# A third up bank for a transformer layer with 64 experts, its opening in another order, and four norms moved to VectorE

## What is computed

```
e    = [fine[id], softmax(cluster logits[id] + b) @ coarse]        # 64 + 64 features
x1   = layernorm(e);  xn = rmsnorm(x1)
x2   = x1 + s1 * (decayed causal q k' v over the 512 tokens) o     # linear attention
h2   = e + x2 + s2 * gelu(rmsnorm(x2) read mix + bias) write       # two residuals
x3   = layernorm(h2)
gate = top 6 of softmax(x3 router), normalised; an expert takes at most 768 tokens in all
y    = h2 + mean of 2 shared experts(x3) + sum over 64 experts of gate * expert(x3)
expert(x) = (silu(x gate_w) * (x up_w)) down_w                     # 128 -> 64 -> 128
```

## Time and profile before

| | |
|---|---|
| median of three runs | 720.69 us |
| profiled execution, its own time | 720.98 us |
| its span in the trace | 719.1 us |
| TensorE products busy | 686.6 us, 95% |
| VectorE busy | 538.4 us, 75% |
| ScalarE busy | 450.4 us, 63% |
| GpSimd busy | 414.8 us, 58% |

### The profile page before, as it was taken

The page is one execution under the profiler, slowest core; times in us unless marked ns, Lnnn a source line. Parts: engine busy times, 40 slices in busy tenths (PEclk is TensorE's granted clock), DMA queues, the critical chain, the costliest instruction groups (busy, mean ns, idle before and its releaser), DMA issues.

```text
span 719.1 us, 10657 instructions
## 1 busy us (share of the span) xinstructions
PE 686.6 (95%) x3264; PEld 549.3 (76%) x3264; DVE 538.4 (75%) x1191; ACT 450.4 (63%) x790; POOL 414.8 (58%) x344
## 2 busy tenths in 40 slices
PE   8877998999999999999999999999999999999998
PEld 7766776788777877778777887778777788778885
DVE  5767689878778787887778787787878776786665
ACT  3345575576675676666765766766766747745554
POOL 5035567565655766565665656557575446556563
PEclk9989999999999999999999999999999999999999
DMA  5402543243223433333332533334332333344441
GB/s 199 167 1 94 159 126 106 93 141 111 103 90 114 127 112 99 113 111 103 114 108 80 147 111 97 111 113 120 112 97 101 114 112 115 94 116 132 140 125 51
DMA packets 49018, 80.54 MB, mean 112 GB/s; under 512 B 9537, under 2 KB 13761, under 8 KB 48961
## 3 DMA queue, kind: packets, MB, share of 16 engines
q1 hardware_dynamic: 47936, 77.76, 34.3%
q0 software_dynamic: 1024, 2.10, 1.6%
HBM read 76.68 MB, written 3.15 MB: 111 GB/s over the span
## 4 chain that ended last, share of the span: by engine, by line
PE 53%; DVE 15%; issue 14%; POOL 13%; ACT 2%; DMA 1%; POOLq 0%; DVEq 0%
POOL hid L1119 11%; PE bank_u L497 5%; PE bank_u L499 5%; PE bank_u L498 5%; PE bank_y L490 5%; PE bank_y L488 5%; PE bank_y L487 5%; PE bank_g L498 5%; PE bank_g L499 5%; PE bank_g L497 5%; DVE bank_u L965 3%; DVE hid_lo L971 3%; DVE taken L905 1%; POOL inv L1096 1%; PE bank_f L425 1%
## 5 line engine op out<-in xcount | busy, mean ns | idle before, releaser
L1119 POOL TENSOR_TENSOR hid<-hid,gate_rows 128x512 f32<-128x512 f32 x256 | 335.3, 1312 | 250.0 <-ACT hid L680 240.1
L688 ACT ACTIVATE hid_hi<-bank_u 128x512 fp32r<-128x512 f32 x259 | 154.6, 597 | 209.0 <-DVE bank_u L965 204.2
L971 DVE TENSOR_TENSOR hid_lo<-bank_u,hid_hi 128x512 fp32r<-128x512 f32 x259 | 178.0, 687 | 96.7 <-ACT hid_hi L688 93.6
L965 DVE TENSOR_TENSOR bank_u<-hid,bank_u 128x512 f32<-128x512 f32 x259 | 178.7, 690 | 47.7 <-PE bank_u L499 39.6
L680 ACT ACTIVATE hid<-bank_g 128x512 f32<-128x512 f32 x264 | 157.3, 596 | 4.3 <-PE bank_g L499 4.0
L497 PE MATMUL bank_u<-x_hi,up_hi 128*128 128x512 f32 x264 | 116.8, 442 | 13.2 <-DVE hid_lo L971 13.1
L497 PE MATMUL bank_g<-x_hi,gate_hi 128*128 128x512 f32 x264 | 106.6, 404 | 0.2 <-issue 0.2
L498 PE MATMUL bank_g<-x_hi,gate_lo 128*128 128x512 f32 x264 | 104.8, 397 | 0.0
L499 PE MATMUL bank_u<-x_lo,up_hi 128*128 128x512 f32 x264 | 104.8, 397 | 0.0
L498 PE MATMUL bank_u<-x_hi,up_lo 128*128 128x512 f32 x264 | 104.5, 396 | 0.0
L499 PE MATMUL bank_g<-x_lo,gate_hi 128*128 128x512 f32 x264 | 104.2, 395 | 0.0
(11 more groups left out here) (223 smaller groups left out, 820.9 us busy)
## 6 DMA issues: line engine op xcount, KB each, us to landing
gate_rows<-gates_dram SPq DMA_DIRECT2D x512, 128.0 KB, 2.9
out_dram<-later SPq DMA_DIRECT2D x7, 256.0 KB, 3.1
hid<-gate_t_dram SPq DMA_DIRECT2D x2, 704.0 KB, 5.8
gates_dram<-gates_t SPq DMA_DIRECT2D x8, 128.0 KB, 2.2
gate_rows<-up_t_dram SPq DMA_DIRECT2D x1, 704.0 KB, 5.6
later<-up_t_dram SPq DMA_DIRECT2D x1, 704.0 KB, 8.6
...
```

The source lines that it names most:

```text
L688: act.activation(hid_hi[:, split_slot(b, p), :], bank_u[(PAIRS * b + p) % 2][:, :], ACT.Copy)\
L965: dve.tensor_tensor(u, h, u, ALU.mult).then_inc(sem("product"), 1)
L971: dve.tensor_tensor(hid_lo[:, k, :], bank_u[(PAIRS * b + p) % 2][:, :], hid_hi[:, k, :].bitcast(F32), ALU.subtract).then_inc(sem("hid_lo"), 1)
L1119: pool.tensor_tensor(hid[:, s, :], hid[:, s, :], gate_rows[:, row, :], ALU.mult).then_inc(sem("gated"), 1)
```

## The change

- Banks: three `bank_u`, one `bank_y`. `up` of pair p waits for `hid_lo` of pair p - 3. The first down product of a batch waits until ScalarE has copied out the sum of the batch before; that copy stands at the start of ScalarE's pair 3 (it stood at pair 5), and at pair 3 TensorE's gate product stands ahead of its down product.
- Norms: `xn`, `x1`, `xn2` and `x3` of every batch are made by VectorE, four tensor_scalar instructions each, as batch 0's were; `scaled` is gone. GpSimd's offsets are still made.
- Opening: the down chunk 0 gets a buffer of its own, is loaded with the first, and is split at pairs 3 and 5 of batch 0; the last up chunk is loaded in its place later. Pair 0 is taken unsplit too (`LATE` = 6). GpSimd halves the shared experts' part behind `inv3`. TensorE does gates 0 to 3 and ups 0 to 2 before the gate transposes, and the transposes of `xn` of batch 1 ahead of them; VectorE does the products of pairs 0 and 1 and `xn` of batch 1 ahead of the token scan. In batch 0 the front-end stages 0 to 7 are done in pairs 0 to 3 (`DENSE`), and gates up to pair 7 and ups up to pair 5 are issued there.
- `hx` on GpSimd is two instructions of half the size, at pairs 12 and 13; `x1` shares memory with weights no longer needed.

```diff
--- before.py
+++ after.py
@@ -45,7 +45,7 @@
 SPLIT_RING = 3
-LATE = 5
+LATE = 6
@@ -57,9 +57,9 @@
              exp_t=9, coarse=10)
-ACT_AT = dict(xn=(-2, -1), xn_hi=0, x1=(1, 3), y_hi=2, z=4, ffn_t=5, xn2=(11, 12), xn2_t=13, vals=14, x3=(19, 20),
-              x3_hi=21, router_exp=23, cluster_exp=8, exp_t=10)
-POOL_AT = dict(inv2=10, hx=12, inv3=18, inv1=17)
+ACT_AT = dict(xn_hi=0, y_hi=2, z=4, ffn_t=3, xn2_t=13, vals=14, x3_hi=21,
+              router_exp=23, cluster_exp=8, exp_t=10)
+POOL_AT = dict(inv2=10, hx=(12, 13), inv3=18, inv1=17)
@@ -74,22 +74,24 @@
           ("up", 0, "rows", -20, 7),
-          ("gate", CHUNK, "hid1", 1, 10),
-          ("up", CHUNK, "later", 3, PAIRS + 3),
+          ("gate", CHUNK, "hid1", 1, 11),
+          ("up", CHUNK, "later", 3, PAIRS + 4),
           ("gate", 2 * CHUNK, "own0", 3, PAIRS + 14),
-          ("up", 2 * CHUNK, "own1", 5, PAIRS + 18),
-          ("down", 0, "rows", 10, 12),
+          ("down", 0, "own1", PAIRS + 3, PAIRS + 5),
+          ("up", 2 * CHUNK, "own1", PAIRS + 16, PAIRS + 18),
...
 FIRST_LOADS = 6
-RELOADS = {6: (1, None), 7: (3, 6), 8: (4, 17)}
+RELOADS = {6: (5, 7), 7: (3, 6), 8: (4, 17)}
...
 SHIFT = 7
-AHEAD = 3
-
-
-WARM = {-1: 8, 1: 12, 3: 9, 5: 7, 7: 36, 12: 3, 13: 4, 17: 24, PE_AT["gates_t"]: 6}
-WARM_START, WARM_PREP, WARM_EXP, WARM_COARSE, WARM_GATES = 20, (2, 9), 4, 26, 20
+AHEAD = 4
+GATES_BEFORE = 8
+DENSE = {0: (0, 1), 1: (2, 3), 2: (4, 5), 3: (6, 7), 4: (), 5: (), 6: (), 7: ()}
+
+
+WARM = {-1: 8, 1: 12, 3: 9, 5: 7, 7: 36, 12: 3, 13: 4, 17: 24}
+WARM_START, WARM_PREP, WARM_EXP, WARM_COARSE, WARM_GATES = 20, (2, 9), 4, 26, 8
@@ -225,9 +226,10 @@
         bank_g = [bank(f"bank_g{i}") for i in range(2)]
-        bank_u = [bank(f"bank_u{i}") for i in range(2)]
-        bank_y = [bank(f"bank_y{i}") for i in range(2)]
+        bank_u = [bank(f"bank_u{i}") for i in range(3)]
+        bank_y = bank("bank_y")
         bank_f = [bank(f"bank_f{i}") for i in range(2)]
+        bank_s = [bank_y, bank_u[2]]
@@ -242,11 +244,15 @@
-            return b == 0 and 1 <= p <= LATE
+            return b == 0 and p < LATE
...
-            return PAIRS * b + p + 1 - (LATE if b or p else 0)
+            return PAIRS * b + p + 1 - LATE
+
+        def stages(b, p):
+
+            return DENSE.get(p, (p,)) if b == 0 else (p,)
@@ -470,16 +475,20 @@
+            if b and p == 0:
+                pe.wait_ge(sem("ffn_t"), b)
...
                 pe.wait_ge(sem("h"), 2)
-            if b == 0 and p % CHUNK == 0:
-                pe.wait_ge(sem(f"split_lo{CHUNK_OF['down', p]}"), 1)
-            y = bank_y[b % 2][:, :]
+            if b == 0 and p in (LATE, CHUNK, 2 * CHUNK):
+                pe.wait_ge(sem(f"split_lo{CHUNK_OF['down', p // CHUNK * CHUNK]}"), 1)
+            y = bank_y[:, :]
             if is_late(b, p):
-                if p == 1:
-                    pe.wait_ge(sem("late_down"), 16)
-                pe.wait_ge(sem("gated"), gated_count(b, p))
-                pe.matmul(y, late_down[:, p - 1, :], hid[:, slot(b, p), :], start=False, stop=False)\
+                if p == 0:
+                    pe.wait_ge(sem("shared_down"), 2)
+                    pe.wait_ge(sem("late_up"), 1)
+                else:
+                    pe.wait_ge(sem("gated"), gated_count(b, p))
+                pe.matmul(y, late_down[:, p, :], hid[:, slot(b, p), :], start=(p == 0), stop=False)\
@@ -506,12 +515,12 @@
-            q, old = PAIRS * b + p, before(b, p, 2)
+            q, old = PAIRS * b + p, before(b, p, 3)
             if old and is_late(*old):
-                pe.wait_ge(sem("late_up"), old[1])
+                pe.wait_ge(sem("late_up"), old[1] + 1)
...
                 pe.wait_ge(sem("hid_lo"), split_count(*old))
-            expert_in(pe, "up", bank_u[q % 2][:, :], b, p)
+            expert_in(pe, "up", bank_u[q % 3][:, :], b, p)
@@ -523,23 +532,38 @@
             for p in range(PAIRS):
-                if p >= AHEAD or not first:
+                if p >= LATE or not first:
                     up(pe, b, p)
+                g = p + GATE_AHEAD
+                if p == LAG and not first:
+                    gate(pe, b, g)
                 if p >= LAG:
-                    down(pe, b, p - LAG)
+                    if not (first and p == LAG):
+                        down(pe, b, p - LAG)
...
                     down(pe, b - 1, p - LAG + PAIRS)
-                g = p + GATE_AHEAD
-                if AHEAD <= g < PAIRS or (g < AHEAD and not first):
+                if GATES_BEFORE <= g < PAIRS or (g < GATES_BEFORE and p != LAG and not first):
...
                     pe_out(pe, b - 1)
-                if late:
-                    pe_late(pe, b + 1, 1 - par, p, early)
+                if first and p == 0:
+                    gate(pe, 0, 4)
+                    up(pe, 0, 4)
+                    gate(pe, 0, 5)
+                elif first and p == 1:
+                    up(pe, 0, 5)
+                    gate(pe, 0, 6)
+                    down(pe, 0, 0)
+                elif first and p == 2:
+                    gate(pe, 0, 7)
+                for q in stages(b, p):
+                    if late:
+                        pe_late(pe, b + 1, 1 - par, q, early)
+                    if early:
+                        pe_early(pe, b + 2, q)
                 if early:
-                    pe_early(pe, b + 2, p)
@@ -593,14 +617,16 @@
                         up(pe, 0, k)
-                    warm(pe, bank_y[1], WARM_GATES)
+                    gate(pe, 0, AHEAD - 1)
+                    pe.wait_ge(sem("h"), 2)
+                    warm(pe, bank_y, WARM_GATES)
+                    pe.wait_ge(sem("router_logits"), 1)
+                    pe_late(pe, 1, 1, PE_AT["xn_t"], False)
...
                 if p == PE_AT["gates_t"]:
-                    gate(pe, 0, AHEAD - 1)
                     up(pe, 0, AHEAD - 1)
-                pe_early(pe, 1, p - SHIFT, bank_y)
-                warm(pe, bank_y[1] if p >= PE_AT["gates_t"] else bank_u[1], WARM.get(p, 0))
-            pe_late(pe, 1, 1, PE_AT["xn_t"], False)
+                pe_early(pe, 1, p - SHIFT, bank_s)
+                warm(pe, bank_u[1], WARM.get(p, 0))
@@ -612,30 +638,8 @@
-        def scaled(act, dst, src, scale, offset, half):
-
-            for t in (2 * half, 2 * half + 1):
-                if offset is None:
-                    last = act.activation(dst[:, t, :], src[:, t, :], ACT.Copy, scale=scale[:, t:t + 1])
-                else:
-                    last = act.activation(dst[:, t, :], src[:, t, :], ACT.Identity, bias=offset[:, t:t + 1],
-                                          scale=scale[:, t:t + 1])
-            return last
-
...
             f0, f1 = bank_f
-            if b and p in ACT_AT["xn"]:
-
-                act.wait_ge(sem("inv1"), b + 1)
-                scaled(act, xn, emb[par], inv1[:, 1, :], off1[:, 1, :], ACT_AT["xn"].index(p)).then_inc(sem("xn"), 1)
-            if b and p in ACT_AT["x1"]:
-                scaled(act, x1, emb[par], inv1[:, 0, :], off1[:, 0, :], ACT_AT["x1"].index(p)).then_inc(sem("x1"), 1)
-            if b and p in ACT_AT["xn2"]:
-                act.wait_ge(sem("inv2"), b + 1)
-                scaled(act, xn2, x2, inv2[:, :], None, ACT_AT["xn2"].index(p)).then_inc(sem("xn2"), 1)
-            if b and p in ACT_AT["x3"]:
-                act.wait_ge(sem("inv3"), b + 1)
-                scaled(act, x3, h2[par], inv3[:, :], off3[:, :], ACT_AT["x3"].index(p)).then_inc(sem("x3"), 1)
@@ -684,32 +688,34 @@
             if old >= 0:
-                act.wait_ge(sem("down_done"), old + (LATE if old else 0) + 1)
-            act.activation(hid_hi[:, split_slot(b, p), :], bank_u[(PAIRS * b + p) % 2][:, :], ACT.Copy)\
+                act.wait_ge(sem("down_done"), old + LATE + 1)
+            act.activation(hid_hi[:, split_slot(b, p), :], bank_u[(PAIRS * b + p) % 3][:, :], ACT.Copy)\
...
-        def act_copy_out(act, b, par):
+        def act_copy_out(act, b):
             act.wait_ge(sem("down_done"), PAIRS * b + PAIRS)
-            act.activation(ffn_t, bank_y[par][:, :], ACT.Copy).then_inc(sem("ffn_t"), 1)
+            act.activation(ffn_t, bank_y[:, :], ACT.Copy).then_inc(sem("ffn_t"), 1)
...
                 n = p + SILU_AHEAD
-                if n < PAIRS and not (first and n < 2):
+                if p == ACT_AT["ffn_t"] and not first:
+                    act_copy_out(act, b - 1)
+                if n < PAIRS and not (first and n <= LATE):
...
                     act_silu(act, b + 1, n - PAIRS)
-                if p == ACT_AT["ffn_t"] and not first:
-                    act_copy_out(act, b - 1, 1 - par)
-                if late:
-                    act_late(act, b + 1, 1 - par, p)
-                if early:
-                    act_early(act, b + 2, p)
-                    act_late(act, b + 2, par, p - PAIRS)
+                for q in stages(b, p):
+                    if late:
+                        act_late(act, b + 1, 1 - par, q)
+                    if early:
```

(84 more changed lines are left out.)

16 lines of the change are left out of this document (8 added, 8 removed).

## The result

The changed kernel takes **726.6 us** (median of 4 runs, 725.1 to 731.0) where the kernel before takes 721.0 in the same session: ratio 1.0085, 95% interval 1.0057 to 1.0113. The forecast of 701 us and its range of 690 to 714 are missed, and the change goes the other way. The profiled execution of after has a span of 723.3 us, before 719.1.

The account below looks back on a forecast made before the run. TensorE was taken to set the pace, held by waits for up banks and x3. Gains of 13.2 (third bank, net of norms), 3.8 (opening) and 2.5 us (pairs 0 to 8), 19.5 in all, gave 701 us, range 690 to 714.

Parts of the forecast that it names:

- What is lost in a batch: In a steady batch TensorE loses 3.0 us to waits for an up bank, x3 and xn, restarts included.
- What the third bank removes: Of 3.0 us lost per steady batch 1.2 stay, 0.8 at x3 and 0.4 at xn; gain 1.8 a batch.
- Rival (1): In steady batches the wait only moves to x3 and gate products, leaving 0.8 us gain per batch: 709 us, chance 0.19.
- The norms on VectorE: Per batch 3.9 us of work plus 3.2 of port waits, less 2.0 in gaps: 5.1 against 6.2 of room.
- L435 waiting over 1.2 us: Sign that the forecast is wrong: TensorE's x3 transposes wait longer than 1.2 us, top of the 0 to 1.2 range.
- groups of four norms lasting over 2.5 us: Sign that the forecast is wrong: VectorE's four tensor_scalar instructions, 1.11 us end to end before, take over 2.5 us.
- rival (4): VectorE becomes the bound through the port; a batch loses 3.5 us: 735 us, chance 0.08.
- The output bank: Single output bank's copy between batches delays down products by 0 to 0.7 us per batch; taken as 0.
- Opening: Until the first gate product: GpSimd's power 2.0 us sooner and TensorE's clock full; gain 3.8 us, product near 48.9.
- Pairs 0 to 8: In batch 0's first nine pairs, 6.3 of 8.8 us waiting and filler stay: gain 2.5, bounds -1.5 to 5.
- two chunk loads together in front of gate rows: With a delayed scan without return, the case behind the low bound of -1.5 us for batch 0's pairs 0 to 8.
- The 2.8 us of gain forecast for these pairs: In batch 0's other 24 pairs the third bank takes 1.8 + 1.0 = 2.8 us.

Follow-up runs that it names:

- the best kernel: Changed kernel with norms of batches 1 to 7 on ScalarE, x3 and xn earlier, later batch 0 loads, batch-after-next's statistics and power earlier: 700.54 us, 0.9708.
- the one with the old opening and the same moves: Kernel before, two up banks, with x3, xn and the batch-after-next's statistics and power moved earlier, but not the loads: 712.38 us, 0.988.
- the trace at 712.7 us: Changed kernel with norms of batches 1 to 7 on ScalarE, x3 and xn earlier and later batch 0 loads: 717.54 us, 0.9956; this execution 712.7.

## Why the prediction was wrong, point by point

The trace of after is 23.7 us longer than the forecast would have it (19.5 + 4.2). The five steady batches hold 11.9 of them (a gain of 9.0 forecast, 2.85 lost), batch 0's pairs 9 to 32 7.8 (2.8 and -5.02), pairs 0 to 8 1.7, batch 7, for which nothing was put, 1.0, batch 6 0.8 and the opening 0.6.

**What is lost in a batch: right.** I counted 3.0 us of waits (the terms that I listed add up to some 3.2); the batch without them takes 79.95 us, so 83.24 - 79.95 = 3.29 were lost.

**What the third bank removes: the step that failed.** All waits for L971 went. The step is "Of the 3.0 us lost per batch I leave 1.2", 0.8 at x3 and 0.4 at xn. Left were 83.53 - 79.95 = 3.58 us. At x3 the sum did let TensorE come 1.0 us earlier, but it had the four norms ready 52.6 to 53.8 us into the batch, before ScalarE's 54.2. They were ready at 54.6, and the wait was 1.85 us. At xn the chain wasn't followed at all: TensorE came ahead by what pairs 26, 27 and 30 no longer wait, xn didn't, and 0.90 us of wait came (L378). So the old waits and the new ones are not stalls in a row: while TensorE stood before the bank, VectorE, GpSimd and ScalarE worked towards x3 and xn, and these come at the same time whether TensorE waited or not (53.29 and 53.33, 81.90 and 81.94). Rival (1) named this, and gave it 0.19; its argument against, that pairs 26 to 31 don't hang on x3, overlooked that they hang on xn in the same way, and it too kept a gain of 0.8 us a batch where 0.29 were lost.

The runs take the 3.58 us off in three steps: 0.97 with GpSimd kept out of x3's group (82.56), 1.48 with x3, xn and the powers moved as well (81.08), 1.13 with the norms back on ScalarE (79.95). That the bank is worth 1.77 us a batch in this last order, close to the 1.8 forecast, is luck: the 1.8 were meant for the order of the change, and there the bank gives nothing (83.28 with the old norms).

**The norms on VectorE: total about right, distribution wrong.** I took 3.9 us of work and 3.2 of port waits in four groups, 7.1 together; VectorE's busy time in batch 3 rose by 6.88 (64.72 to 71.60). The groups for x1 and x3 last 2.71 and 2.96 us, 1.60 and 1.85 over the 1.11 of the earlier trace rows, those for xn and xn2 only 1.49 and 1.30; so most of the price lies in two groups, and is not spread over four. I put x3's new wait at 0.8 us within 0 to 1.2; 1.85 of idle time came, because x3 starts just when GpSimd gates two pairs on end. The upper bound had it behind one product of GpSimd; the group met two, and the signs "L435 waiting over 1.2 us" and "groups of four norms lasting over 2.5 us" had it. The rule quoted there from the Trainium skill ("SBUF — State Buffer", "Who interferes with whom") was the right one to weigh: with GpSimd kept out, the same four take 1.11 us. What the norms on VectorE cost a batch hangs on the other meetings: 0.25 us in the change (83.53 against 83.28), 1.0 in the kernel before, 1.13 in the best order, but 3.4 with x3 one pair earlier (85.55 against 82.19, part of it a lowered clock), near rival (4)'s 3.5.

**The output bank: cost put at 0, right in steady batches of after, not elsewhere.** It took 1.0 us in batch 7 (pair 3: 3.13 us for 2.10) and 0.8 a batch where the meetings were moved later: the upper bound of 0.7 was a little low.

**Opening: right.** 3.25 us for 3.8, first gate product 49.41 for 48.9, GpSimd's power at 34.83 where it stood at 36.64, and the clock at 1.00 from 38.00 to 44.80 where the earlier trace rows have 0.50. Each is one execution: in the traces of the experiments the first gate product comes at 49.16 to 50.71 us with the new opening and at 52.21 to 53.22 with the old, and the granted clock of that stretch is 0.91 to 1.00 and 0.59 to 0.75.

**Pairs 0 to 8: 0.81 us for 2.5, and what follows lost.** The low end of that range named a cause, "two chunk loads together in front of gate rows", which struck just behind those pairs: GpSimd waited 2.39 and 2.10 us for gate rows at 80.94 and 84.33, and pairs 9 and 10 took 10.97 us (6.10 before), nearly all of the 5.02 that the other 24 pairs lost. Moving both loads gave 2.9 and 4.4 us back; moving one gave none. The 2.8 us of gain forecast for these pairs failed like the steady batches: pairs 17 to 20 take 12.61 us in after and 12.57 before, with one wait of 3.67 us at x3 in place of 1.52 and 0.74 for the bank and 0.83 at x3.

**Open.** The whole new opening leads by 4 us at the tenth up product, but the best kernel starts batch 1 only 1.2 us ahead of the one with the old opening and the same moves (142.27, 143.46), and in these 1.2 us its third bank and its later loads are included. Which meeting of batch 0 keeps the rest was not separated.

## What to carry to other kernels

A wait that an engine spends on one resource may be the time in which the others make its next input: before pricing its removal, follow the next meeting back through the other engines and ask whether its time depends on the wait at all. Here the bank gave nothing in a steady batch, and the norms and the earlier x3 lost, as long as the next meeting kept its time; the same bank gave 1.77 us a batch once x3, xn and GpSimd's power stood where they were needed. Of a step moved up in a queue, count what filled its old waiting time and now stands behind it.

## What the chip showed beyond that

A short pause can cost more than its length. In batch 4 of after TensorE waits at x3 as in batch 3, but 1.4 us later its clock is granted at 0.50, the lower of 1.2 and 2.4 GHz, for 3.41 us, and the batch takes 84.78 us in place of 83.53. The wait, and the stretch in the form of the stages above:

```profile
454.35 0.66 PE L440 MATMUL bank_f<-ident,xn 128*128 128x128 f32 x4 [1.85 <-DVE xn L850]
```
```profile
455.77:459.18 3.41, 3.41 (x13) 2.92 (x12) 2.58 (x4) 2.92 (x6) 1.65 (x2) 0.50 0.16 52
```

In the run with one reload later three steady batches take this 1.2 us more (84.73 to 84.99). The two runs of x3 made earlier on VectorE have a granted clock of 0.96 to 0.98 in every steady batch, where TensorE pauses 1.42 and 1.48 us at pair 21; the runs with 82.56 and 79.95 us a batch, without pauses above 1 us there, have 1.00 in all. But the same 1.85 us leaves the clock at 1.00 in batches 1, 2, 3 and 5 of after, and 1.48 us at pair 21 do so in every steady batch of the trace at 712.7 us: what decides is not shown. The ten executions of that kernel lie at 712.7 to 714.8 us with a mean clock of 0.988 to 0.993 and at 720.2 to 722.2 with 0.978 to 0.980; whether such stretches make this difference is not shown either, as the one trace is of the first kind.
